# The dense graph layer: front sums in 16 pieces behind even chunks, back products in two PSUM banks

## The reference

```python
ei = concatenate([edge_index, stack([loops, loops])], axis=1)   # every node also has an edge to itself
col, row = ei[0], ei[1]
ew = inv_sqrt(out_deg)[row] * inv_sqrt(in_deg)[col]
y_forward  = segment_sum((x @ W_f.T)[row] * ew[:, None], col)    # "front", 128 features
y_backward = segment_sum((x @ W_b.T)[col] * ew[:, None], row)    # "back", 128 features
y = concatenate([y_forward, y_backward], axis=-1) + bias_param
```

## Time and profile before

| | us |
|---|---|
| three runs | 5373.17, 5383.99, 5381.75 |
| median | 5381.75 |
| span of the profiled execution, first to last instruction | 5371.9 |
| of it the dense stage | about 3303 to 4640 |
| PE, DVE, ACT busy in the whole span | 4172.9, 3413.4, 1663.0 |

### The profile page before, as it was taken

One profiled execution on the slowest core, in us unless ns is written; L12 is line 12 of the kernel. 1 busy time (PEld: TensorE's weight loads), 2 busy tenths in 40 slices (PEclk: granted clock), 3 DMA queues, 4 the chain that ended last, 5 costly groups with the idle time before them and its releaser, 6 DMA issues. The chain is left out here.

```text
span 5371.9 us, 86748 instructions
## 1 busy us (share of the span) xinstructions
PE 4172.9 (78%) x27330; PEld 3017.8 (56%) x27331; DVE 3413.4 (64%) x7289; ACT 1663.0 (31%) x2903; POOL 2167.4 (40%) x2194
## 2 busy tenths in 40 slices
PE   3477777777777777746999945999999999769992
PEld 2355555555555555534888833666656666458872
DVE  6466666666666666687555577888888888640115
ACT  1233333333333333321222264333333333121121
POOL 1477777777777777700666600000000000202220
PEclk9678777777777887756999966999999999759996
DMA  4766666666666666651566543444444444323333
GB/s 122 189 168 170 167 165 170 170 162 170 170 165 167 170 169 163 158 207 68 193 200 199 183 139 84 81 85 89 81 81 88 87 81 85 88 86 121 100 118 103
DMA packets 946866, 733.83 MB, mean 137 GB/s; under 512 B 703102, under 2 KB 832054, under 8 KB 944599
## 3 DMA queue, kind: packets, MB, share of 16 engines
q1 hardware_dynamic: 835851, 433.62, 31.3%
q0 software_dynamic: 104144, 289.95, 20.0%
q10 hardware_dynamic: 6652, 7.32, 0.4%
HBM read 483.39 MB, written 92.34 MB: 107 GB/s over the span
## 5 line engine op out<-in xcount | busy, mean ns | idle before, releaser
L1288 POOL DMA_INDIRECT gat_rows<-h_rows,gat_sources x1664 | 1577.0, 948 | 509.2 <-issue 485.5
L1526 PE MATMUL gat_sum_ps<-gat_rows,gat_onehot 128*128 128x265 f32 x3328 | 1167.6, 510 | 3.2 <-DVE gat_rows L1418 2.4
L1526 PEld LDWEIGHTS gat_sum_ps<-gat_rows,gat_onehot 128*128 128x128 f32 x3328 | 792.9, 250 | 190.4 <-issue 5.7
L2055 ACT CAST gnn_z<-build_ps 128x392 bf16<-128x392 f32 x992 | 473.4, 486 | 847.7 <-PE build_ps L2070 842.3
L1997 DVE TENSOR_TENSOR onehot_low<-dense_codes,dense_iota_bf 128x2048 bf16<-128x2048 bf16 x496 | 604.0, 1218 | 2.6 <-PE build_ps L2070 2.6
L2080 PE MATMUL back_ps<-zb_pieces,gnn_z 128*128 128x384 bf16 x3038 | 567.1, 327 | 0.0
L2102 PE MATMUL front_ps<-x_res_wide,front_rows 128*128 128x448 bf16 x2604 | 562.5, 353 | 0.0
L1976 POOL DMA_INDIRECT front_rows<-zf_piece_rows,vrow_nodes x62 | 64.8, 1046 | 1231.2 <-PE front_ps L2102 1221.0
L1418 DVE TENSOR_TENSOR gat_rows<-gat_rows,gat_numerators_ps 128x1024 f32<-128x1024 f32 x416 | 502.0, 1207 | 0.0
L2471 PE MATMUL moe_hidden_ps<-moe_rows_T,moe_w 128*128 128x256 f32 (+1 forms) x1408 | 459.9, 483 | 2.7 <-DVE moe_rows_T L2512 0.8
L2070 PEld LDWEIGHTS build_ps<-onehot_high,onehot_low 128*128 128x128 bf16 x7936 | 339.4, 98 | 204.6 <-issue 38.5
(11 more groups left out here) (366 smaller groups left out, 5160.4 us busy)
## 6 DMA issues: line engine op xcount, KB each, us to landing
moe_w<-in_L_ffn_W SPq DMA_DIRECT2D x112, 512.0 KB
gat_targets<-gat_step_targets SPq DMA_DIRECT2D x104, 512.0 KB
moe_w<-in_L_ffn_w SPq DMA_DIRECT2D x32, 1024.0 KB
gat_rows<-h_rows,gat_sources POOLq DMA_INDIRECT x1664
moe_rows_out<-moe_slot_zeros SPq DMA_DIRECT2D x36, 512.0 KB
gat_flags<-gat_tile_flags SPq DMA_DIRECT2D x104, 128.0 KB
normal_rows<-moe_xn_all SPq DMA_DIRECT2D x14, 896.0 KB
mid_taken<-moe_rows_out SPq DMA_DIRECT2D x14, 896.0 KB, 7.3
```

What stands on the lines that cost most here:

```text
L1288: pool.indirect_dma_start(out=g[:, b, t, :], out_offset=None, in_=T.h[:, :], in_offset=bass.IndirectOffsetOnAxis(ap=idx[:, b, t:t + 1], ax ...
L1526: last = pe.matmul(po[:, s % BANKS, 0:W], o[:, b, s * SUB + t, :], g[:, b, s * SUB + t, :], start=t == 0, stop=t == SUB - 1)
L2055: nc.scalar.copy(AT[:, k % 2, :, CHUNK * c:CHUNK * (c + 1)], pb[:, c % 2, 0:CHUNK * NT].rearrange("p (u h) -> p h u", u=CHUNK)).then_inc(a ...
```

## The change

The number of front pieces `PARTS` is now the number of chunks, 16 a pair and so 8 a slot, each of 392 columns (`CN` = 49 x 128 / 16), still 6 matmuls each. They move from the odd chunks 1 to 13 to the even chunks 0 to 14. The seven back groups move from the even chunks 2 to 14 to the odd chunks 1 to 13. The merge moves from chunk 1 of a slot to chunk 15, behind that slot's last build, so it comes 14 chunks later. `back_ps` has two banks, one for each parity of the unit, and the first back group waits for the sum of back of two units before, not of one. On DVE `sum_back` is called for chunk 13 where it was 14, and `add_back` for chunk 15 where it was 1.

```diff
--- before.py
+++ after.py
@@ -1885,7 +1885,7 @@
     DUO = 2
     HITS = 2
     PAIRS = CHUNK * DUO // HITS
-    PARTS = 2 * NT // GROUP
+    PARTS = NC
     CN = NT * P // PARTS
     AHEAD = 4
     HALF = PARTS // 2
@@ -1916,7 +1916,7 @@
         i2_i = k.sb(ctx, "iota_wide_int", [P, 2 * P], I32)
         i2 = k.sb(ctx, "iota_wide", [P, 2 * P])
         pb = k.ps(ctx, "build_ps", [P, 2, 512])
-        py = k.ps(ctx, "back_ps", [P, 512])
+        py = k.ps(ctx, "back_ps", [P, 2, 512])
         pm = k.ps(ctx, "merge_ps", [P, 512])
         pf = k.ps(ctx, "front_ps", [P, 2, 512])
         block = ctx.enter_context(nc.Block())
@@ -1940,7 +1940,7 @@
         def front_at(k, c):
 
             first = k % 2
-            return (c - 1) // 2 + (0 if first else HALF), (k - 3 if first else k - 4) % SLOTS
+            return c // 2 + (0 if first else HALF), (k - 3 if first else k - 4) % SLOTS
 
         @block.sync
         def _(sp):
@@ -2001,8 +2001,8 @@
                 last.then_inc(oh, 1)
 
             def add_front(q, k, c):
-                f = q * HALF + ((c - 1) // 2 - 3 * HALF)
-                n = (k * HALF + (c - 1) // 2 - 3 * HALF) % 2
+                f = q * HALF + (c // 2 - 3 * HALF)
+                n = (k * HALF + c // 2 - 3 * HALF) % 2
                 at = front_at(k, c)[0] * CN
                 dve.wait_ge(yf, f + 1)
                 until(dve, ya, f - (PARTS - 1) if k >= 5 else 0)
@@ -2013,7 +2013,7 @@
                 dve.wait_ge(yb, q)
                 until(dve, mg, q - 2)
                 dve.tensor_scalar(mrg[:, n, :], i2[:, :], C.vlocal[:, bass.ds(q - 1, 1)], None, ALU.is_equal)
-                dve.tensor_reduce(ybv[:, n, :], py[:, 0:3 * P].rearrange("p (s f) -> p f s", s=3), AX.X,
+                dve.tensor_reduce(ybv[:, n, :], py[:, k % 2, 0:3 * P].rearrange("p (s f) -> p f s", s=3), AX.X,
                                   ALU.add).then_inc(yr, 1)
 
             def add_back(q, k):
@@ -2024,12 +2024,12 @@
                 dve.tensor_tensor(rows, rows, pm[:, 0:2 * P], ALU.add).then_inc(md, 1)
 
             def sums(q, k, c):
-                if c == 1 and 2 <= k <= NQ + 1:
+                if c % 2 == 0 and 3 <= k <= NQ + 2:
+                    add_front(q, k, c)
+                if c == 2 * GROUP - 1 and 1 <= k <= NQ:
+                    sum_back(q, k)
+                if c == NC - 1 and 2 <= k <= NQ + 1:
                     add_back(q, k)
-                if c % 2 and c <= 2 * HALF - 1 and 3 <= k <= NQ + 2:
-                    add_front(q, k, c)
-                if c == 2 * HALF and 1 <= k <= NQ:
-                    sum_back(q, k)
 
             def slot(q, r, k):
                 for c in range(NC):
@@ -2074,10 +2074,10 @@
             def back(q, k, g):
                 if g == 0:
                     pe.wait_ge(ae, q * NC)
-                    until(pe, yr, q - 1)
+                    until(pe, yr, q - 2)
                 for n in range(GROUP):
                     h = g * GROUP + n
-                    last = pe.matmul(py[:, 0:3 * P], AT[:, (k - 1) % 2, h, :], zb3[:, h, :, :].rearrange("p s f -> p (s f)"),
+                    last = pe.matmul(py[:, k % 2, 0:3 * P], AT[:, (k - 1) % 2, h, :], zb3[:, h, :, :].rearrange("p s f -> p (s f)"),
                                      start=h == 0, stop=h == NT - 1)
                 if g == GROUP - 1:
                     last.then_inc(yb, 1)
@@ -2091,12 +2091,12 @@
                 last.then_inc(mg, 1)
 
             def front(q, r, k, c):
-                if c == 1 and k % 2:
+                if c == 0 and k % 2:
                     pe.wait_ge(te, q * 16 - 16)
                     pe.wait_ge(zg[0 if k % BODY == 3 else 1], r * 32 + (32 if k % BODY == 3 else 0))
                 chunk, first = front_at(k, c)
-                n = (k * HALF + (c - 1) // 2 - 3 * HALF) % 2
-                until(pe, ya, q * HALF + ((c - 1) // 2 - 3 * HALF - 1))
+                n = (k * HALF + c // 2 - 3 * HALF) % 2
+                until(pe, ya, q * HALF + (c // 2 - 3 * HALF - 1))
                 for s in range(2):
                     for m in range(3):
                         last = pe.matmul(pf[:, n, 0:CN], zfv[:, first + s, m * P:(m + 1) * P],
@@ -2108,12 +2108,12 @@
                 for c in range(NC):
                     if k < NQ:
                         build(q, k, c)
-                    if c % 2 == 0 and c and 1 <= k <= NQ:
-                        back(q, k, c // 2 - 1)
-                    if c == 1 and 2 <= k <= NQ + 1:
+                    if c % 2 == 0 and 3 <= k <= NQ + 2:
+                        front(q, r, k, c)
+                    if c % 2 and c // 2 < GROUP and 1 <= k <= NQ:
+                        back(q, k, c // 2)
+                    if c == NC - 1 and 2 <= k <= NQ + 1:
                         merge(q, k)
-                    if c % 2 and c <= 2 * HALF - 1 and 3 <= k <= NQ + 2:
-                        front(q, r, k, c)
             supersteps(pe, slot, 3)
```

## The result

The changed kernel takes 5291.39 us (median of 4 runs, 5287.98 to 5293.19) where the kernel before, with a fourth run, takes 5381.84 (5373.17 to 5383.99). The ratio is 0.9833, 95% interval 0.9819 to 0.9847: 90 us less. The prediction was 5297, range 5284 to 5322. A later measurement gave 5284.24 beside 5374.63, again 0.9833.

What follows compares the result with a forecast made beforehand. PE was taken to bound the dense stage, so its removed waits come off the span. 53.0 + 30.7 + 1.5 - 0.8 = 84.4 us off the 5381.75 median gave 5297.3, range 5284 to 5322.

Steps and rivals of the forecast that it cites:

- Merge behind the last build, 53.0 us: Slot edge on PE: the merge's wait for DVE's sum of back goes with its drain, 61 x 0.87 us.
- the clock, 1.5: Near the stage's start: without the first merge's wait PE's fall to clock 0.50 goes, 1.5 us gained, between 0 and that.
- Front in even and back in odd chunks, 30.7 us: Builds 15, 0 and 1 on PE: products or the merge between builds remove the wait for ACT's copy, 59 x 0.52.
- Two banks, nothing: First back group, now at chunk 1: one bank would wait for this edge's sum, two ask one slot earlier; no cost.
- Finer pieces, 0.8 us lost: Front matmuls on PE: 372 more at 2.1 ns each beyond their columns, 0.8 us lost, between 0 and 3.7.
- DMAs: Transfer for the front piece at chunk 0: lands 10.6 us after issue, issued 19.9 us before the piece; no cost.
- A slot of 17.95 us: DVE's work in one slot: one-hots, eight additions, the sum of back and the addition of merged rows, without the new wait.
- the new idle of 0.87: DVE in front of the sum of back: waits 0.87 us for the back group of chunk 13.
- cover is left: DVE after the slot edge: 1.8 us late at piece 0, yet 1.8 to 2.2 us remain before PE waits.
- rival 3: DVE's lateness reaches PE, 0.7 us beyond the cover in each slot, gives back 41 us: 5338; chance 0.05.
- rival 5: Slower, DVE becomes the bound at 21.9 us a slot: slots 0.6 longer, 38 us, so 5420; chance 0.04.
- 5288 as its lower bound: Fast end of the working: a gain of 85.2 us, with runs before reaching 8.6 below their median.

Runs made afterwards that it cites:

- experiment 8: The kernel before with the merge and its addition at chunk 3 instead of 1, nothing else: 5318.30 us, ratio 0.9896.
- experiment 3: The changed kernel with one bank of back instead of two, its first group waiting for the sum of one unit before: 5288.84 us, ratio 0.9832.
- experiment 5: The changed kernel with each front piece computed as four quarters of 98 columns: 5317.54 us, ratio 0.9892.
- experiments 6 and 7: The changed kernel with more sums of back a slot on DVE, to a spare tile: two more 5290.84 us, four more 5341.27 us.
- experiment 1: The kernel before with only the merge moved behind the last build and its addition following: 5293.94 us, ratio 0.9840.
- experiment 4: The changed kernel with 14 front pieces of 448 columns, in even chunks 2 to 14: 5290.13 us, ratio 0.9833.

## Why the prediction was right, and where it was off

**What bounds.** PE, and a us that it does not wait is a us off the span: 89.9 us of stage, 90 of median.

**Merge behind the last build, 53.0 us, and the clock, 1.5.** Right in kind. The merge at chunk 3 alone gave 55.2 for 54.5, but in part by luck: its slots are 0.80 shorter than before and not 0.87, some 49 us in 61 of them, and the slots where the loop turns, 5.3 us over the usual before and 2.0 in that run, gave 3.3, which the sum did not have. In the changed kernel's trace the dip near the start of the stage is gone, as said: the first front piece of the stage shows 1.15 us where the earlier trace rows had 2.22.

**Front in even and back in odd chunks, 30.7 us.** Right in kind. The sizes per slot can be read from the starts of the merges: 21.23 before, 20.43 with the merge at chunk 3, 19.82 in the changed kernel. So the merge's wait is worth 0.80 where I had 0.87, and what goes with ACT's 0.61 where I had 0.52. The start of build 1 is late by 0.52, as worked out. Of the other 0.09, 0.05 is the late start of the front piece behind a build that had waited, 0.08 in every second slot (experiment 8), which I charged nowhere; in the kernel before it lies inside the wait of the merge, and shows only when that is gone. The last 0.04 is spread thinly over the other builds. In sum it is 1.41 a slot for 1.39. In slot 2, which has no front pieces yet, ACT's wait stayed, 0.5 us once.

**Credit to parts.** The prediction gave each part a share: merge 53, chunks 31, the bank nothing. For the merge and the chunks, each taken alone, this does not hold. The merge's move alone is worth 84.7 and the chunks' alone 89.8. The merge's move also parts the builds, and the chunks' move also puts DVE's sum ahead of a pair of one-hots and a front piece of cover between edge and merge. The sum was right because the two waits were both removed, not because each edit removed its own; for either edit alone these prices would have missed by 30 and by 59 us.

**Two banks, nothing.** Right, by experiment 3. The reason given was not: with one bank the first back group does ask for the sum of this very edge, but that sum ends at 3903.67 and the group starts at 3905.91 in the changed kernel, so one bank waits for nothing either.

**Finer pieces, 0.8 us lost.** By experiment 5 2.6 ns a matmul, 1.0 us. The Trainium skill, page "TensorE: Matmul & The Clock Gate", section "Wait — 56ns, not 53.3ns?", which the prediction weighed, has about 2.5 ns; this case's measure agrees with it.

**DVE.** A slot of 17.95 us was forecast and 17.7 measured; the new idle of 0.87 is 0.80 to 0.84. DVE adds piece 8 as the first one on time (3916.19), four rounds behind piece 0, as worked out. That cover is left was right, and experiments 6 and 7 say how much: 1.06 us at no cost, 2.25 us at 0.80 a slot. Neither a PE that waits for DVE in each slot (rival 3) nor a slot set by DVE (rival 5) is in the changed kernel's trace.

**DMAs.** The transposing transfer lands 11.3 us after its issue in the changed kernel, and no engine waits for it in a slot of 19.82.

**The sum.** 84.4 forecast, 89.9 in the stage. Of the 5.5 missing, about 1.4 lie ahead of slot 3. From the first build to that of chunk 15 in slot 2 it is 37.96 us where it was 39.88, 1.9 less, and the forecast had 0.5 there. PE's rows, the first two before and the last two after:

```profile
3318.00 2.42 PE L2080 MATMUL back_ps<-zb_pieces,gnn_z 128*128 128x384 bf16 x7
...
3320.91 2.11 PE L2080 MATMUL back_ps<-zb_pieces,gnn_z 128*128 128x384 bf16 x7
...
3323.65 2.42 PE L2080 MATMUL back_ps<-zb_pieces,gnn_z 128*128 128x384 bf16 x7
...
3326.38 1.30 PE L2080 MATMUL back_ps<-zb_pieces,gnn_z 128*128 128x384 bf16 x7
```

PE waits there for the one-hots of each pair of builds, and the first back group now stands one chunk earlier: it starts 13.48 after the first build, where it was 14.76. It runs at the lower clock in both (granted 0.50). The second one still did before (2.11 long) and does not now (1.30). Another 0.5 of the 1.9 is no gain: the merge of slot 2 has only moved behind that build.

Where the loop turns, the slots are 3.9 us over the usual and were 5.3, another 1.4, and where it ends one slot was 0.4 over the usual and is not now: the prediction left these stops out of the sum. The 0.03 a slot by which the difference of two slots was set too low (1.38 after the cost of the finer pieces, for 1.41) are 1.8. That makes 5.0; the last half us I do not place.

**The range.** The working has 5288 as its lower bound, and the range begins at 5284, for which it gives no term. The measured 5291 lies inside both.

## What to carry to other kernels

Before pricing a wait by its idle time, look at the starts of the groups on both sides: the drain ahead of it and the late restart behind it are on the path too (here 0.36 idle was 0.52 by the starts, and 0.60 in every second slot). When a piece of work is moved, ask of every wait near its old and its new place whether it changes, not only of the one it is moved for; three short products in a row on two buffers wait for the copy, and one item between two of them ended that here, the 0.53 us merge between the first two or a 0.99 us front piece between the last two. And try the smallest edit alone: here one statement moved on PE, with its addition on DVE, gave 94% of what four coupled edits gave, the second bank gave nothing, and the finer pieces 1 to 2 us at most.

## What was not expected of the hardware

A front piece directly behind the pair of builds 0 and 1 starts 0.08 us late in every second slot and not in the others: 0.51 and 0.44 from the pair's start in experiment 1, 0.30 and 0.225 from build 1's in experiment 8. A back group in the same place is at 0.44 in every slot (experiment 4). All of them have build 1 at the least distance from ACT's copy. The late ones are the slots of odd `k`, in which the piece of chunk 1 is the first of a pair and `front` has two more waits ahead of it, for the turned unit and for the gathered rows. No wait of PE is put to either. In the changed kernel the same two waits stand behind build 0, which waits for nothing, and the piece follows it after 0.21 in both kinds of slot. So it seems that waits that are long met cost time only behind a build that has itself just been released. That is read from the pattern; no run moved these two waits alone.
